# Masked mixing matrices, a new order of the first phase's maxima and turns, and the last tile's raw rows beside the second matrix's tiles

## The reference, cut to what matters

```python
x = x + ffn0(mix(x, cond))       # block 0
x = x + ffn1(conv(x, cond))      # block 1

def mix(x, emb):
    h = gelu(gelu(emb @ W0 + b0) @ W1 + b1)
    att = softmax(h @ W2 + b2)                       # (64 batches, K = 8)
    agg_w = einsum('bk,koi->boi', att, weight)       # a 64x64 matrix for each batch
    return einsum('boi,bih->boh', agg_w, x) + (att @ bias_k)[:, :, None]

def ffn0(x, weight, bias):                           # fp8 with one scale for a whole tensor
    sx, sw = max(abs(x)) / 448, max(abs(weight)) / 448
    return (fp8(x / sx) @ fp8(weight.T / sw)) * (sx * sw) + bias

def ffn1(x, W_q, scale, zero, bias):                 # 4-bit weights, groups of 128
    return x @ ((W_q - zero) * scale).T + bias       # fp16
```

## Time and profile before

| What | us |
| --- | --- |
| median of 3 runs (lowest, highest) | 527.69 (527.61, 528.54) |
| the profiled execution | 527.88 |
| its span in the profile | 526.1 |
| TensorE busy | 511.2 |
| VectorE busy | 414.4 |
| ScalarE busy | 243.9 |
| GpSimd busy | 59.3 |

### The profile page before, as it was taken

One profiled execution on the slowest core, in us unless ns is written; L12 is line 12 of the kernel. 1 busy time (PEld: TensorE's weight loads), 2 busy tenths in 40 slices (PEclk: granted clock), 3 DMA queues, 4 the chain that ended last, 5 costly groups with the idle time before them and its releaser, 6 DMA issues.

```text
span 526.1 us, 9556 instructions
## 1 busy us (share of the span) xinstructions
PE 511.2 (97%) x3528; PEld 286.0 (54%) x3528; DVE 414.4 (79%) x526; ACT 243.9 (46%) x286; POOL 59.3 (11%) x68
## 2 busy tenths in 40 slices
PE   5799999999999999999999999999999999999997
PEld 4544444355555555555555555555555555555564
DVE  6899999877887777777777777777777777777652
ACT  3479897754344444444444444444444444442310
POOL 5276666020000000000000000000000000000000
PEclk9999999999999999999999999999999999999999
DMA  7999681235675655566666565555566656565632
GB/s 225 393 386 405 222 329 42 80 82 142 185 218 182 181 181 181 181 181 181 181 181 181 181 181 181 181 181 181 182 183 182 182 183 180 183 185 186 199 122 80
DMA packets 85795, 100.61 MB, mean 191 GB/s; under 512 B 34484, under 2 KB 67318, under 8 KB 85782
## 3 DMA queue, kind: packets, MB, share of 16 engines
q1 hardware_dynamic: 84754, 99.41, 59.2%
q0 software_dynamic: 656, 0.82, 0.9%
q10 hardware_dynamic: 372, 0.20, 0.1%
HBM read 58.41 MB, written 32.75 MB: 173 GB/s over the span
## 4 chain that ended last, share of the span: by engine, by line
PE 81%; DVE 11%; issue 2%; DMA 2%; SPq 1%; ACT 1%; POOL 1%; DVEq 0%; ACTq 0%; POOLq 0%
PE pair L1190 41%; PE pair L1164 19%; PE pair L1180 16%; DVE stat L805 5%; DMA Y<-in_L_ffn_weight_dram 2%; PE pair L1154 1%; PE pair L1064 1%; DVE work L730 1%; DVE work L820 1%; DVE Y L820 1%; DVE work L733 1%; PE pair L1267 1%; SPq L337 1%; POOL fixed L490 1%; DVE work L742 1%
## 5 line engine op out<-in xcount | busy, mean ns | idle before, releaser
L1190 PE MATMUL pair<-f1T,work 128*128 128x512 f16 x1008 | 227.5, 379 | 0.0
L1190 PEld LDWEIGHTS pair<-f1T,work 128*128 128x128 f16 x1008 | 97.2, 98 | 111.7 <-DVE work L929 0.2
L609 ACT ACTIVATE work<-Y,consts 128x1024 bf16 (+1 forms) x29 | 33.3, 1149 | 185.7 <-DVE work L903 185.7
L922 DVE TENSOR_TENSOR work<-Y,work 128x512 f16<-128x512 f16 (+1 forms) x64 | 71.2, 1120 | 47.2 <-ACT work L642 46.3
L1164 PE MATMUL pair<-f0T,work 128*128 128x512 bf16 x464 | 104.9, 379 | 0.0
L1180 PEld LDWEIGHTS pair<-taps,work 128*128 128x128 f16 x1536 | 88.3, 98 | 8.0 <-issue 0.5
L1180 PE MATMUL pair<-taps,work 128*128 128x128 f16 x1536 | 91.0, 219 | 0.0
L642 ACT CAST work<-Y 128x512 f16 (+1 forms) x64 | 69.5, 1136 | 18.6 <-DVE Y L912 15.6
L935 DVE TENSOR_TENSOR Y<-pair,Y 128x512 f32 (+1 forms) x63 | 43.3, 687 | 41.3 <-PE pair L1190 41.3
L1164 PEld LDWEIGHTS pair<-f0T,work 128*128 128x128 bf16 x464 | 45.3, 98 | 54.8
L1064 PE MATMUL pair<-Y,work 128*128 128x512 f32 x128 | 60.6, 608 | 0.4 <-ACT Y L582 0.4
(11 more groups left out here) (161 smaller groups left out, 251.5 us busy)
## 6 DMA issues: line engine op xcount, KB each, us to landing
Y<-in_x_dram SPq DMA_DIRECT2D x64, 512.0 KB, 3.9
out_dram<-Y SPq DMA_DIRECT2D x31, 512.0 KB, 3.7
split_rows<-work SPq DMA_DIRECT2D x30, 520.0 KB, 2.6
work<-split_rows SPq DMA_DIRECT2D x30, 520.0 KB, 3.9
Y<-in_L_ffn_weight_dram SPq DMA_DIRECT2D x8, 512.0 KB, 7.3
Y<-in_L_ffn_W_q_dram SPq DMA_DIRECT2D x5, 512.0 KB, 14.2
work<-in_L_ffn_W_q_dram SPq DMA_DIRECT2D x3, 512.0 KB, 15.2
work<-work SPq DMA_DIRECT2D x8, 65.0 KB, 3.7
```

What stands on the lines that cost most here:

```text
L922: nc.vector.tensor_tensor(split[:, r, s, 1], v[:, r, :], split[:, r, s, 0], ALU.subtract)\
L1190: last = mm(ps[2 + h][:, :], y1s[n][:, e, k, :], f1T[:, k, h * H:(h + 1) * H], start=False, stop=(e == 1 and k == KT - 1), skip_group_chec ...
```

## The change

In order of the kernel:

- **Mixing matrices.** The bf16 parts and their DMAs are gone. `wkf` is now (8 x 16) = 128 rows of 256 columns, loaded by GpSimd's queue first of all. The attention is repeated 16 times along its row (`attR`), transposed once, and multiplied with a mask `own_c` (which row belongs to which of the 16 groups) into `attM`, 128 x (16 x 64) f32, in two halves. Four f32 matmuls of 512 columns give the mixing matrices. The bias matrix `mbk2` has 128 rows, of which every sixteenth is loaded and the rest is zero.
- **Idle matmuls.** They read a cleared row (`idle_rows`): five of 512 columns at the start, then 2, 16 and 8 of 128; 12 and 10 others are gone.
- **VectorE's order.** The maxima of W0 all stand behind the attention; the tap sums are moved ahead; the maxima of tiles 0, 1 and 2 are taken during the exchange of W0's maximum; the groups of the cycles are a new list.
- **TensorE's and ScalarE's order.** turned0(r) stands behind tile 3r + 9 (the last one behind tile 31), turned1(n) behind tile 3n + 10 for n up to 5, and turned1(6) and turned1(7) behind all tiles. The two steps of W0's maximum stand behind tile 3 and within tile 4 instead of 0 and 1. `scale_w0(r)` now stands behind tile 3r + 2 for r from 1 to 7.
- **Loads.** x tiles 0 and 1 stand further ahead, 21 and 22 stand before 16; the last tile's raw rows go in two halves into `work`, behind w1i(5) and w1i(6), and no longer wait for slot 31. A wait on `moved_sp` ahead of a later load is gone.
- **GpSimd.** Window loads stand ahead of the rounding loop; the `b0` and `b1` rows stand ahead of the clearing of the pads.

```diff
+        def last_raw(h):
+            return work[:, (5 + h) * L + H:(6 + h) * L]
...
+        KC = P // K
+        KR = K * KC
+        wkf = work[0:KR, 5 * L:5 * L + KF]
+        attM = work[0:KR, 6 * L:6 * L + KC * B].rearrange("p (c b) -> p c b", c=KC)
+        idle_rows = f1T[:, 0, 0:H]
...
-        groups = [(0, 1)] + [g for r in range(R8) for g in ((3 * r + 1, 2), (3 * r + 3, 1))]
-        groups += [(25, 2), (27, 2), (29, 1), (30, 1), (31, 1)]
-        groups[-1:] = [(31, 0), (31, 1)]
+        beside = [[(0, 1), (1, 1)], [(2, 1)]]
+        cycle_groups = [[(3, 2), (5, 2)], [(7, 2), (9, 2)], [(11, 2), (13, 2)], [(15, 2), (17, 2)], [(19, 2), (21, 2)],
+                        [(23, 2), (25, 1)], [(26, 2), (28, 1)], [(29, 2), (31, 0), (31, 1)]]
+        groups = [g for c in beside + cycle_groups for g in c]
...
-        turns0 = {3 * r + 6: r for r in range(R8)}
-        turns1 = {3 * n + 8: n for n in range(KT)}
+        turns0 = {3 * r + 9 if r < R8 - 1 else T - 1: r for r in range(R8)}
+        turns1 = {3 * n + 10: n for n in range(KT - 2)}
...
+        turn_order += [("w1", KT - 2), ("w1", KT - 1)]
...
             for r in range(3):
                 load_w0(r)
-            for e in range(2):
-                sp.wait_ge(wk_parts, (1, 3)[e])
-                for i in range(3):
-                    sp.dma_start(wkp9[3 * i + e:KP:9, :], wkp[:, e, :]).then_inc(ld["wkp"], 16)
             load_w0(3)
+            load_mixing(0)
+            sp.wait_ge(mbk_zero, 1)
...
             load_w0(5)
-            load_mixing(0)
+            load_mixing(1)
             load_w0(6)
             load_w0(7)
...
             load_mixing(15)
+            sp.wait_ge(taps_split, 4)
+            load_mixing(21)
+            load_mixing(22)
             for t in range(16, 21):
                 sp.wait_ge(w1_less, t - 15)
                 load_mixing(t)
...
-            for r in range(R8):
+            for r in range(R8 - 1):
                 sp.wait_ge(w0q, r + 1)
                 if r < 2:
                     sp.wait_ge(wT_mm, turn_at("w1", 3 + r) + 1)
                 load_mixing(W0_SLOT + r)
+            for h in range(2):
+                sp.wait_ge(w1_less, 6 + h)
+                sp.dma_start(last_raw(h), x_t[T - 1, :, h * H:(h + 1) * H]).then_inc(ld_x[T - 1], 16)
...
             move(0)
             sp.wait_ge(first_q, 6)
-            sp.wait_ge(moved_sp[1], 32)
             load_x(2, 0)
...
                     act.wait_ge(mixed, t + 1 + h)
+                    if t == T - 1:
+                        act.wait_ge(w0q, R8)
...
-                if t % 3 == 2 and t <= 20:
-                    scale_w0(t // 3 + 1)
+                if t % 3 == 2 and 5 <= t <= 23:
+                    scale_w0(t // 3)
...
+            for n in (KT - 2, KT - 1):
+                keep_w1(n)
             keep_sums(0)
...
+            nc.vector.memset(idle_rows, 0.0).then_inc(idle_zero, 1)
+            clear_mixw(0)
+            clear_mixw(1)
+            dve.wait_ge(ident_made, 1)
+            nc.vector.tensor_reduce(own_c, ident[0:KR, 0:KR].rearrange("p (k c) -> p c k", k=K), AX.X, ALU.add)\
+                .then_inc(own_made, 1)
+            clear_mixw(2)
+            clear_mixw(3)
...
-            largest_w0(0)
             dve.wait_ge(mlp_mm, 4)
             nc.vector.tensor_reduce(nmax, ps[3][0:B, 0:K], AX.X, ALU.max, negate=True).then_inc(mlp_ev, 1)
...
+            for h in range(2):
+                c = slice(h * KC // 2, (h + 1) * KC // 2)
+                nc.vector.tensor_tensor(attM[:, c], ps[6][0:KR, 256:256 + B].unsqueeze(1).to_broadcast([KR, KC // 2, B]),
+                                        own_c[:, c].unsqueeze(2).to_broadcast([KR, KC // 2, B]), ALU.mult)\
+                    .then_inc(mlp_ev, 1)
...
+            largest_w0(0)
+            largest_w0(1)
             dve.wait_ge(ld["convw"], 32)
             dve.wait_ge(tapcols_made, 3)
             for part in (tapsum, tapsum2):
                 nc.vector.tensor_reduce(part, convraw.rearrange("p c k -> p k c"), AX.X, ALU.add)\
                     .then_inc(tapsum_red, 1)
+            place_last()
+            for r in range(2, R8):
+                largest_w0(r)
+            dve.wait_ge(w_red, R8)
+            nc.vector.tensor_reduce(w_part, w_rows, AX.X, ALU.max).then_inc(w_red, 1)
+            largest_mixed(0)
+            largest_mixed(1)
             dve.wait_ge(w_pe, 1)
             nc.vector.tensor_reduce(w_all, ps[7][0:1, 0:P], AX.X, ALU.max).then_inc(w_red, 1)
+            largest_mixed(2)
             dve.wait_ge(w_pe, 2)
...
                 less_w1(r)
-                if r == 0:
-                    largest_mixed(0)
-                largest_mixed(2 * r + 1)
-                largest_mixed(2 * r + 2)
-            for n in range(2 * R8 + 1, NGRP):
-                largest_mixed(n)
+                for g in cycle_groups[r]:
+                    largest_mixed(groups.index(g))
...
+            keep_clock(8)
+            pe.wait_ge(ld["wk"], 16)
+            for h in range(2):
+                pe.wait_ge(mlp_ev, 8 + h)
+                for m in range(2):
+                    last = mm(ps[2 * h + m][:, :], wkf[:, m * 2 * C:(m + 1) * 2 * C],
+                              attM[:, h * KC // 2:(h + 1) * KC // 2].rearrange("p c b -> p (c b)"),
+                              start=True, stop=True)
+                last.then_inc(mix_mm, 1)
+            turned_tap_rows(range(R8))
...
             for t in range(T):
                 mixed_tile(t)
-                if t == 0:
+                if t == 3:
                     pe.wait_ge(w_red, R8 + 1)
                     nc.tensor.transpose(ps[7][0:1, 0:P], w_part, ident[:, :]).then_inc(w_pe, 1)
...
-            pe.wait_ge(wT_ev, 2 * KT)
+            for n in (KT - 2, KT - 1):
+                turned1(n)
+            pe.wait_ge(wT_ev, 2 * KT - 2)
...
             mm(ps[7][:, 128:129], ones, x_all, start=True, stop=True).then_inc(x_pe, 1)
+            pe.wait_ge(wT_ev, 2 * KT)
             weight_sums(1, range(KT))
```

More of the change, by code:

```diff
@@ L131, in adaln_ffn_kernel @@
         mw2 = mlp[:, 832:840]
-        att = mlp[0:B, 840:848]
-        attT = mlp[0:K, 848:912]
+        attR = mlp[0:B, 840:840 + KR]
+        own_c = mlp[0:KR, 996:996 + KC]
         rowb = mlp[0:1, 976:984]
@@ L453, in _ @@
                 pool.dma_start(convraw[b * C:(b + 1) * C], convw).then_inc(ld["convw"], 16)
+            nc.gpsimd.memset(mbk2, 0.0).then_inc(mbk_zero, 1)
             nc.gpsimd.memset(wide_taps, 0.0).then_inc(taps_zero, 1)
@@ L460, in _ @@
             nc.gpsimd.memset(windowp[:, 2], 1.0).then_inc(windowp_ones, 1)
-            pool.wait_ge(wk_parts, 4)
-            for i in range(3):
-                pool.dma_start(wkp9[3 * i + 2:KP:9, :], wkp[:, 2, :]).then_inc(ld["wkl"], 16)
             pool.wait_ge(ld["convw"], 32)
@@ L1055, in _, with turned_tap_rows @@
-            last.then_inc(taps_mm, 1)
+            nc.tensor.transpose(ps[6][0:KR, 256:256 + B], attR, ident[0:B, 0:B]).then_inc(mlp_mm, 1)
+            def turned_tap_rows(ws):
+                pe.wait_ge(taps_made, 3)
+                for w in ws:
+                    last = nc.tensor.transpose(pair[2][:, w * P:(w + 1) * P],
+                                               taps_rows[:, w].rearrange("p c r -> p (c r)"), ident[:, :])
+                if w == R8 - 1:
+                    last.then_inc(taps_mm, 1)
@@ L1063, in mixed_tile @@
                 for h in range(2):
-                    last = mm(ps[2 * (t % 2) + h][:, :], mixw[:, t, :], slot(t)[:, h * H:(h + 1) * H],
-                              start=True, stop=True)
+                    raw = last_raw(h) if t == T - 1 else slot(t)[:, h * H:(h + 1) * H]
+                    last = mm(ps[2 * (t % 2) + h][:, :], mixw[:, t, :], raw, start=True, stop=True)
                     if h or t == T - 1:
                         last.then_inc(mixed, 1)
-                    if t == 1 and h == 0:
+                    if t == 4 and h == 0:
                         pe.wait_ge(w_red, R8 + 2)
```

159 lines of the change are left out of this document (51 added, 108 removed).

## The result

The changed kernel takes 552.8 us (551.56 to 555.11, 4 runs) against 527.84 beside it (4 runs), a ratio of 1.0472 with an interval from 1.0445 to 1.05: 25 us slower. The profiled execution took 551.56, the shortest of the four, its span 549.6, where the one before had 526.1; why the median is 1.2 us longer no profile shows. The forecast was 547.0, with a range of 541 to 554.

What follows compares the result with a forecast made beforehand. VectorE's maxima, taken without rest, set when the exchange starts; a later head and starved cycles put the maxima's transposition at 112.1 instead of 92.58, 19.5 us later, added to 527.88 (547.4; 547.2 against the median): 547, range 541 to 554.

Steps and rivals of the forecast that it cites:

- Starvation: In cycles 2 to 6 VectorE waits for mixed tiles that come late; cycle 4 takes 16.3 us; chance 0.60.
- the rival of a milder starvation: Tile 20 is there in time; cycle 4 takes 12.0 instead of 16.3 us, total 543; chance 0.10.
- The first rival: TensorE slows in its gaps in cycles 4, 5 and perhaps 6: +5 to +7 us, 553; chance 0.20.
- price of 0.85 a pass: Time of a slowed matmul pass behind a gap, instead of 0.43; puts 1.7 us on tile 20.
- the old trace's 1.00 in every stretch: Granted clock in the profile before the change, taken as evidence against TensorE slowing in the gaps.
- The head: From the start to the first cycle: mixing matmuls start at 11.9, first cycle at 31.0 (29.2 to 32.3) instead of 26.84.
- The exchange: Behind the tiles, where the mixed rows' maximum is exchanged: transposition of the maxima starts at 112.1 us instead of 92.58.
- C7: Start of cycle 7, the last of VectorE's cycles, forecast at 102.3 us.
- the cover of the b0 rows: In the exchange: b0 rows start at turned1(7)'s end, land in some 3 us as fixed_part(0) comes, under 1 us to spare.
- the weight sums' place: Five weight sums stand ahead of the maxima's transposition, formerly done in waiting time: 1.25 us.
- Faster, if nothing starved: Tiles always ahead, first cycle at 29.2: transposition 1.1 us earlier, 526.6; faster 0.05, within no starvation's 0.10.
- L731: Row that opens a VectorE cycle: stays short, 0.42 instead of 0.91, saving 0.5 us in each of five cycles.

Runs made afterwards that it cites:

- x9: The changed kernel with only the list of groups turned back to three tiles' maxima a cycle: 529.94 us, ratio 1.0028.
- x1: The changed kernel with the fifth less_w1 and those behind it a cycle earlier, so that tile 20's slot is free earlier: 548.86 us, ratio 1.039.
- x3: The changed kernel with less_w1 from the fifth on a cycle earlier, and W0 turns and scalings moved one or two mixed tiles back: 535.28 us, ratio 1.0154.
- x4: The changed kernel with 120, 84 and 66 idle matmuls in TensorE's gaps ahead of tile 20 and behind tiles 24 and 27: 547.66 us, ratio 1.0369.
- x7: The changed kernel with the transposition of the maxima ahead of the five weight sums that stood before it: 553.88 us, ratio 1.0483.
- x12: x9 with 50 idle matmuls ahead of tile 20: 526.54 us, ratio 0.9973 to the kernel before.
- x5: x3 with one of cycle 3's two less_w1 put ahead of that cycle's rounding: 534.88 us, ratio 1.013.
- x8: x6 with 50 idle matmuls behind tile 0, where TensorE waits for the maxima of W0: 527.81 us, ratio 0.9999.
- x6: The kernel before the change with the new head alone, cycles and exchange as before: 530.8 us, ratio 1.0044.

## Why the prediction was right

- **Starvation, the forecast's main step**: right, shown by x9, which undoes it alone, and by x1 to x3, which undo its two halves. With tile 20 loaded in time cycle 4 takes 11.65 us (x1), where the rival of a milder starvation had 12.0. Where it sits is right too: waits in cycles 2 and 3, the large one in cycle 4 behind the fifth less_w1 and a landing of 3.27 us (3.2 was used), then 5 and 6 behind the cycle's own rounding. Up to cycle 3 each cycle is within 0.4 us.
- **The first rival**, slowing in the gaps, given 0.20, came on top: cycle 4 1.5, cycle 5 1.3 and cycle 6 2.4 longer than forecast. Its total of +5 to +7 fits x4's 5.1. Its price of 0.85 a pass does not follow from the rows it names, though: 1.89 for 16 against 0.62 for 8 is a ratio of 1.5 and gives 0.65. Half pace is what the runs then showed, 3.43 us for four passes, 0.86 each. The step that failed is the weight given to the old trace's 1.00 in every stretch: it had no long gap in it, so it spoke neither for nor against. In the changed kernel the clock went to its lower level behind gaps of 7.2, 4.8 and 3.8 us. Here the trace agrees with the Trainium skill (TensorE: Matmul & The Clock Gate, "What's actually happening"), cited in the forecast: an idle engine returns to 1.2 GHz, and the next matmuls start there.
- **The head** was sized wrong. The first cycle came at 28.10, forecast 31.0 and bound 29.2. The eight mixing matmuls took 4.06 us from 10.66 on, where 3.5 to 6.8 from 11.9 had been taken, and VectorE made the attention matrix by 11.1, not 12.4. The last maximum of W0 ended at 23.1, below the bound of 24.0: TensorE was slow in the head by no more than 0.51 a pass against 0.45. Of the clock's 5.2 in the cycles, this 2.9 took back more than half: the transposition came 2.2 late. That the measured time lies within 6 us of 547 is so in part luck, two errors of opposite sign.
- **The exchange**: forecast 9.8 from C7 to the transposition, measured 9.5; the cover of the b0 rows was put at "under 1 us" and was none: TensorE waits 0.31 there in the changed kernel, 1.68 in x3 and 1.79 in x7. The forecast had these rows start at turned1(7)'s end; they start 2.3 us behind it (115.48 against 113.15), since GpSimd first loads and casts the b1 row. Whether the 1.25 put on the weight sums' place would be won without this, x7 does not show. The fall of the clock in the first product with W0 (+1.6 to 1.8) was not foreseen.
- **Faster, if nothing starved** (526.6): with the starvation removed, x9 gives 529.94 and x12, with the clock held too, 526.54. That this is the rival's number is luck: its sum runs at four maxima a cycle of 7.75 us from a first cycle at 29.2, those kernels at three a cycle of 7.07 from 28.1 and 28.9. The nearest with four a cycle, x3 and x5, are at 535.28 and 534.88.
- **L731** stays at 0.42, as forecast.

## What to carry to other kernels

Before giving a consumer more items a cycle, write down for each item the last instruction ahead of it on every in-order queue, and when its buffer comes free: a lead of three tiles was eaten in three cycles, and one buffer released in the same cycle in which its tile was wanted made VectorE wait 8.3 us at one place (x1, which frees it a cycle earlier, is 3.9 us faster). A gap on TensorE costs twice, once as a wait and once in the pace of what follows, so look at the granted clock by stretches of a few microseconds; where the gap itself can't be closed, idle matmuls of its length give the second half back (5.1 us in x4, 3.0 in x8 over x6, 3.4 in x12 over x9; by the ratios to the kernel before beside each, 2.4 and 2.9 for the last two). And a part that gets faster alone may give nothing: the head's 1.7 us went to the clock first, then, in the one profile there is, to the landing of a load.
